# One-core attention and mixture-of-experts kernel: a token load, a late weight and leftover pair work change places at the start of the expert steps

## The reference

```python
q = relu(x @ Wq.T + bq); k = relu(x @ Wk.T + bk); v = x @ Wv.T + bv     # 16 heads of 16
q_ = concat([q * sin, q * cos]); k_ = concat([k * sin, k * cos])        # by position
kv = einsum('nld,nlm->ndm', k_, v)
z = 1.0 / maximum(einsum('nld,nd->nl', q_, k_.sum(axis=1)), 1e-4)
x = layernorm(x + (einsum('nld,ndm->nlm', q_, kv) * z) @ Wo.T + bo)
logits = x @ router_w.T; topv, topi = top_k(logits, 2); w = softmax(topv)
for e in range(8):
    out += gate[:, e:e+1] * (gelu(x @ w1[e].T) @ w2[e].T)               # 256 -> 512 -> 256
x = layernorm(x + out)
```

## Time and profile before

| what | value |
|---|---|
| median of 3 runs | 858.84 us (858.13 to 859.87) |
| the profiled execution | 858.07 us |
| its span, first to last instruction | 856.3 us |
| mean granted TensorE clock | 0.981 |
| PE busy | 800.6 us (93%) |
| DVE busy | 566.9 us (66%) |
| ACT busy | 460.2 us (54%) |
| POOL busy | 428.8 us (50%) |
| HBM traffic | 124 GB/s over the span |

### The profile page before, as it was taken

The page is one execution under the profiler, slowest core; times in us unless marked ns, Lnnn a source line. Parts: engine busy times, 40 slices in busy tenths (PEclk is TensorE's granted clock), DMA queues, the critical chain, the costliest instruction groups (busy, mean ns, idle before and its releaser), DMA issues.

```text
span 856.3 us, 22053 instructions
## 1 busy us (share of the span) xinstructions
PE 800.6 (93%) x6684; PEld 736.7 (86%) x6684; DVE 566.9 (66%) x1816; ACT 460.2 (54%) x1044; POOL 428.8 (50%) x545
## 2 busy tenths in 40 slices
PE   5999999999899869999999999999999999999990
PEld 4888999889899858999899999989999999999980
DVE  3336788878888766666766666664444477777773
ACT  3556676666766644445444544434444445566653
POOL 3886566666677663444445444553222234444442
PEclk9999999999999978999999999999999999999996
DMA  6444033333333242332333332232322355666644
GB/s 195 164 139 133 26 115 121 101 102 107 105 101 101 89 154 82 101 96 89 90 102 106 101 98 85 88 107 82 120 76 78 122 186 191 223 224 215 227 168 172
DMA packets 56469, 106.64 MB, mean 125 GB/s; under 512 B 9262, under 2 KB 37552, under 8 KB 54449
## 3 DMA queue, kind: packets, MB, share of 16 engines
q1 hardware_dynamic: 41296, 63.25, 25.0%
q0 software_dynamic: 12624, 33.84, 10.8%
q10 hardware_dynamic: 2448, 8.26, 2.6%
HBM read 61.91 MB, written 44.32 MB: 124 GB/s over the span
## 4 chain that ended last, share of the span: by engine, by line
PE 80%; DVE 6%; issue 5%; ACT 5%; DMA 3%; SPq 1%; POOL 1%; ACTq 0%; POOLq 0%; DVEq 0%
PE PS L736 23%; PE PS L724 22%; PE PS L540 10%; PE PS L754 7%; PE PS L577 4%; PE PS L713 4%; PE PS L613 4%; PE PS L629 3%; PE PS L600 1%; PE PS L560 1%; ACT vs L851 1%; DMA boc<-in_bo_columns 1%; ACT vs L850 1%; PE PS L547 1%; DVE o L1047 1%
## 5 line engine op out<-in xcount | busy, mean ns | idle before, releaser
L1670 POOL DMA_INDIRECT token_rows<-xg x135 | 134.8, 998 | 284.0 <-DVE xg L1403 261.6
L736 PEld LDWEIGHTS PS<-w,hT 128*128 128x128 f32 x1620 | 211.7, 189 | 13.5 <-issue 3.7
L724 PE MATMUL PS<-w,xgT 128*128 x810 | 222.9, 411 | 0.0
L736 PE MATMUL PS<-w,hT 128*128 x1620 | 218.3, 284 | 0.8 <-ACT hT L994 0.8
L724 PEld LDWEIGHTS PS<-w,xgT 128*128 128x128 f32 x810 | 143.8, 191 | 24.3
L1586 POOL DMA_INDIRECT expert_rows<-rows,idx x128 | 131.0, 1024 | 60.1 <-issue 35.4
L994 ACT ACTIVATE hT<-PS 128x512 fp32r<-128x512 f32 x135 | 80.7, 598 | 142.1 <-PE PS L754 138.4
L990 ACT ACTIVATE hg<-PS 128x512 f32<-128x512 f32 x135 | 80.5, 596 | 118.4 <-PE PS L724 106.4
L1468 DVE TENSOR_TENSOR hT<-PS,hT 128x512 fp32r<-128x512 f32 x135 | 93.4, 692 | 75.6 <-ACT hT L994 75.6
L1395 DVE TENSOR_TENSOR xgT<-PS,xgT 128x256 fp32r<-128x256 f32 x135 | 57.0, 422 | 75.6 <-ACT xgT L960 57.6
L754 PE MATMUL PS<-cst,hg 128*128 128x128 f32 x540 | 81.5, 273 | 0.7 <-ACT hg L990 0.7
(11 more groups left out here) (179 smaller groups left out, 1276.5 us busy)
## 6 DMA issues: line engine op xcount, KB each, us to landing
xg<-expert_rows SPq DMA_DIRECT2D x135, 130.0 KB
z<-token_rows SPq DMA_DIRECT2D x15, 1024.0 KB
xraw<-in_xT SPq DMA_DIRECT2D x32, 256.0 KB
xtok<-in_x SPq DMA_DIRECT2D x32, 256.0 KB
out_y<-z ACTq DMA_DIRECT2D x15, 512.0 KB, 3.2
wraw<-in_w1T SPq DMA_DIRECT2D x7, 512.0 KB, 3.8
wraw<-in_w2T SPq DMA_DIRECT2D x7, 512.0 KB, 3.6
token_rows<-xg POOLq DMA_INDIRECT x135
```

The costliest lines, as they stand in the source:

```text
L724: mm = nc.tensor.matmul(PS[:, gH, :], xgT[:, s % 2, a, k, :], w[:, bass.ds(e, 1), b, k * F:(k + 1) * F].rearrange("p o f -> p (o f)"), sta ...
L736: return nc.tensor.matmul(PS[:, gY, 0:D], hT[:, a, k, :], w[:, bass.ds(e, 1), b, HALF + k * D:HALF + (k + 1) * D] .rearrange("p o f -> p ( ...
L1670: nc.gpsimd.indirect_dma_start(yd, bass.IndirectOffsetOnAxis(ap=xg[:, XG_SLOTS[s % NXG], C_DST:C_GATE].bitcast(U32), axis=0), xg[:, XG_SLO ...
```

## The change

Nothing is added or left out of what is computed; only places in the engines' orders change.

- SP: `tokens(23)` moves from ahead of the late weight's first half to behind the eighth gather. In the steps, `tokens(j)` moves from hook place 0 to place 4.
- Last rep of the first phase: DVE does `positions(20)` and `attention_low(22)` at once, and `gates(20)`, `row_stats(21)`, `row_means(21)` and `logits(21)` move behind `rows_low(0)`. POOL does `late_weight` ahead of `half_deviation(21)`, and two of pair 20's four scatters move into steps 0 and 1.
- PE: `attend(23)`, second half, moves behind `hidden(0)`; `rank(21)`, `attention_transposed(23)`, `project_out(23)` and `rank(22)` each one step later.
- ACT: `normalise(21)` and the second cosine part move into step 0, `query_high(24)` into 1, `attention_high(23)` from 2 to 4, `normalise(22)` from 1 to 5, `normalise(23)` from 6 to 8.
- DVE: the blocks of pairs 21 to 23 that lay ahead of the steps and in steps 0 to 5 lie in steps 0 to 7; the `seg_start` part moves from step 5 to step 12.
- POOL: pair 21's scatters go from steps 1 to 4 to steps 3 to 6, the first two of pair 22 from 5 and 6 to 7 and 8, the deviations and gate powers one to three steps later.

```diff
@@ SP
-            tokens(GROUP_PAIRS - 1)
             sp.wait_ge(q_done, NPAIR)
             sp.dma_start(w_late_raw[:, 0, 1, 0:HALF], w_experts[0][EARLY]).then_inc(s_late[0], 16)
@@ SP, steps
             for s in range(FULL_STEPS):
-                if hook(s)[1] == 0 and s < LAST_GROUP:
+                if s == NXG:
+                    tokens(GROUP_PAIRS - 1)
+                if hook(s)[1] == 4 and hook(s)[0] is not None:
                     tokens(hook(s)[0])
@@ PE
             rows_transposed(0)
-            attend(A, G - 1, 1)
@@ PE, steps
                 hidden(s, now)
-                if s == 5:
+                if s == 0:
+                    attend(A, G - 1, 1)
+                if s == 6:
                     rank(A - 1, G - 1, A)
...
-                if s == 0:
+                if s == 1:
                     rank(A - 2, G - 2, A)
-                if s == 2:
+                if s == 3:
                     attention_transposed(A, G - 1)
-                if s == 4:
+                if s == 5:
                     project_out(A, G - 1)
@@ ACT
-            normalise(A - 2, (A - 2) // 2, True, 1)
-            nc.scalar.activation(gelu_first[:], half_neg[:, 0:2], ACT.Gelu, scale=2.0)
             act.wait_ge(s_late[0], 16)
             act.wait_ge(kv_done, 2 * NPAIR)
             nc.scalar.activation(w[:, EARLY, 0, 0:HALF], w_late_raw[:, 0, 1, 0:HALF], ACT.Copy).then_inc(late_high, 1)
             cos_part(A, G - 1, 0)
+            nc.scalar.activation(gelu_first[:], half_neg[:, 0:2], ACT.Gelu, scale=2.0)
...
             rows_high(0)
-            cos_part(A, G - 1, 1)
-            query_high(A + 1, A + 1 - GROUP_PAIRS, True)
@@ ACT, steps
+                if s == 0:
+                    cos_part(A, G - 1, 1)
+                    normalise(A - 2, (A - 2) // 2, True, 1)
                 if s == 1:
+                    query_high(A + 1, A + 1 - GROUP_PAIRS, True)
+                if s == 4:
+                    attention_high(A, G - 1)
+                if s == 5:
                     normalise(A - 1, (A - 1) // 2, True, 0)
-                if s == 2:
-                    attention_high(A, G - 1)
-                if s == 6:
+                if s == 8:
                     normalise(A, A // 2, True, 1)
@@ DVE, first phase
+                if rep == NPAIR - 1:
+                    dve.wait_ge(x1_ready, j - 1)
+                    positions(j - 2, slot)
+                    attention_low(j)
+                    return
@@ DVE
             state_out(B - 1, 2 * NPAIR)
-            choose(A - 2, G - 2, 1)
...
-            residual(A - 1, 0, (A - 1) // 2 * 16 + 16)
-            logits_sum(A - 1, 2 * ((A - 1) % LX))
             add_sin_part(A, G - 1, 0)
...
             rows_low(0)
-            row_stats(A - 1, 0)
-            row_means(A - 1, G - 2)
-            logits(A - 1)
-            add_sin_part(A, G - 1, 1)
-            gates(A - 2, G - 2, 1)
+            row_stats(A - 2, 1)
+            row_means(A - 2, G - 3)
+            logits(A - 2)
+            gates(A - 3, G - 3, 0)
@@ DVE, steps
                 if s == 0:
+                    choose(A - 2, G - 2, 1)
+                    add_sin_part(A, G - 1, 1)
+                if s == 1:
+                    state_split(B - 1)
+                if s == 2:
                     normalise_attention(A, G - 1)
-                    state_split(B - 1)
-                if s == 1:
+                    residual(A - 1, 0, (A - 1) // 2 * 16 + 16)
+                    logits_sum(A - 1, 2 * ((A - 1) % LX))
+                if s == 3:
+                    dve.wait_ge(x1_ready, A - 1)
+                    gates(A - 2, G - 2, 1)
                     positions(A - 2, 1)
-                if s == 2:
+                    row_stats(A - 1, 0)
+                if s == 4:
+                    row_means(A - 1, G - 2)
+                    logits(A - 1)
                     attention_low(A)
+                if s == 5:
+                    choose(A - 1, G - 1, 0)
                     query_low(A + 1, A + 1 - GROUP_PAIRS)
-                if s == 3:
-                    choose(A - 1, G - 1, 0)
-                    gates(A - 1, G - 1, 0)
-                if s == 4:
+                if s == 6:
                     residual(A, 1, A // 2 * 16 + 16)
                     logits_sum(A, 2 * (A % LX))
+                    dve.wait_ge(x1_ready, A)
+                    gates(A - 1, G - 1, 0)
+                    positions(A - 1, 0)
+                if s == 7:
                     row_stats(A, 1)
                     row_means(A, G - 1)
                     logits(A)
-                if s == 5:
-                    positions(A - 1, 0)
+                if s == FIRST_GROUP + GROUP - 1:
@@ POOL, first phase
+                if rep == NPAIR - 1:
+                    late_weight()
                 if onward:
                     half_deviation(j - 1)
...
                 if rep == NPAIR - 1:
-                    late_weight()
                     scattered(j - 2)
-                    for h in range(2):
-                        for k in range(TOPK):
-                            scatter(slot, h, k)
+                    scatter(slot, 0, 0)
+                    scatter(slot, 0, 1)
@@ POOL, steps
-            gate_power(A - 2)
-            half_deviation(A - 1)
...
-                if 1 <= s <= 4:
-                    if s == 1:
+                if s < 2:
+                    scatter(0, 1, s)
+                if s == 1:
+                    gate_power(A - 2)
+                if 3 <= s <= 6:
+                    if s == 3:
                         scattered(A - 2)
-                    scatter(1, (s - 1) // 2, (s - 1) % 2)
+                    scatter(1, (s - 3) // 2, (s - 3) % 2)
                 j, n = hook(s)
-                if s == 3:
+                if s == 4:
+                    half_deviation(A - 1)
+                if s == 5:
                     gate_power(A - 1)
...
+                if s == 7:
+                    half_deviation(A)
                 send(s)
-                if s == 4:
-                    half_deviation(A)
-                if 5 <= s <= 6:
-                    if s == 5:
+                if 7 <= s <= 8:
+                    if s == 7:
                         scattered(A - 1)
-                    scatter(0, 0, s - 5)
+                    scatter(0, 0, s - 7)
```

## The result

The changed kernel took **851.41 us** in the median of 9 runs, the kernel before 858.84: a ratio of 0.9926, with a 95% interval of 0.9908 to 0.9944. The profiled execution took 851.41 us, its span is 849.6 us at a mean granted clock of 0.984 (before: 858.07, 856.3, 0.981).

The account below looks back on a forecast made before the run. TensorE bounds the kernel, idle where attention ends and expert steps begin. 6.3 - 0.76 + 0.7 + 0.65 - 0.5 = 6.4 us off the median 858.84 gives 852.4 us; range 850.0 to 856.8.

Parts of the forecast that it names:

- The chain to the first expert product: Transition from attention to expert steps: earlier weight and gather bring the first expert product to 314.7 instead of 321.04.
- The scatter's completion: Pair 19's last scatter, which the first gather awaits: taken as complete at 309.5, bounds 309.0 and 311.7.
- the rival of the late confirmation: Scatter complete only at 311.7: transition slides 2.2 us, gain 4.2, 854.6 us; chance 22%.
- the estimate of 311.0: Scatter's completion with the skill's roughly 2 us, mostly write receipt, counted from data end; sum 1.5 us worse, 853.9 us.
- that term: Transition up to the first expert product, at 314.7 instead of 321.04: gain 6.3 us.
- Attention product: Pair 23's second half on TensorE moves behind the first expert product: 0.76 us given back.
- gelu gap: TensorE's 0.69 us wait for ScalarE's gelu, covered by the moved attention product: gain 0.7 us.
- clock: Half speed lasts 3.4 to 6.8 us behind the first expert product's start; middle cost 2.5: gain 0.65 us.
- stalls: Extra work spread over eight steps instead of six, TensorE gaps of at most 0.3 us: 0.5 us given back.
- The token load's place: Token loads at the fourth hook, not the zeroth: gathers no longer queue behind them; worth 0.
- my number for GpSimd's whole part of the weight: Late weight's second half on GpSimd: 3.9 us of its own after the last scatter, ending at 311.9.

Follow-up runs that it names:

- e6: Changed kernel without GpSimd's wait for the attention division ahead of pair 19's last two scatters, last rep only: 849.68 us, ratio 0.991.
- e2: Kernel before with only the late weight's first half loaded ahead of pair 23's token load: 854.41 us, ratio 0.9971.
- e3: Kernel before with late weight and gathers ahead of pair 23's token load, now behind seven gathers; other engines keep the old order: 855.84 us, ratio 0.9978.
- e4: Changed kernel with the late weight's first half loaded right behind the first gather: 857.9 us, ratio 1.0009.
- e8: Changed kernel with 32 small matmuls added on TensorE ahead of the first expert product, shifting its code: 852.8 us, ratio 0.9958.
- e10: Changed kernel with GpSimd's second scatter of pair 23's first half moved from step 8 to step 9: 846.66 us, ratio 0.9927.
- e5: Changed kernel with VectorE's state split moved back from step 1 to step 0: 854.39 us, ratio 0.9968.
- e9: Changed kernel with the steps' token load back at hook place 0 instead of 4: 854.86 us, ratio 1.002.
- e11: Changed kernel with pair 23's second-half attention product back ahead of the first expert product on TensorE: 846.1 us, ratio 0.9923.
- e7: e6 with ScalarE's gelu table loaded in the last rep and VectorE's sin part behind its first rows: 849.33 us, ratio 0.9914.
- e1: The changed kernel as it is, run and profiled again on another chip: 852.95 us, ratio 0.9945.
- e12: e7 with gather 0's transposes ahead of pair 22's output projection on TensorE: 851.02 us, ratio 0.9925.

## Why the prediction was right, and where it was not

**The chain to the first expert product** held link by link. Predicted and measured: weight issued 301.2 and 301.41; rounding 307.2 and 307.21; gather 310.6 and 310.66; transposes 312.7 and 312.84; product 314.7 and 314.84. The scatter's completion, which no row of before showed, is 309.6 where I took 309.5: SyncE's last wait ahead of the gathers, at the line of the earlier trace rows, now begins at 305.4 and lasts 4.23 us, and in e6, where the scatters go out earlier, 0.03 us:

```profile
L466 SPq EVENT_SEMAPHORE  x1: 4233/4233/4233, 305.4 to 305.4; - x1
```

That refutes the rival of the late confirmation and the estimate of 311.0 that I had drawn from the Trainium skill (DMA: Bandwidth & Descriptors, the anatomy of a GpSimd DMA); the receipt was in by 2.5 us after the scatter's issue at 307.12. e2, e3 and e4 show how the parts hang together. The early weight load is worth 2.9 us, the early gathers nothing on top of it, and the gathers with the other engines' new orders 3.1; with the weight late, all the rest is worth 1.7. What the old order leaves late once both loads are early is ScalarE's rounding of the weight as well as VectorE's extra blocks (e3).

**The size of that term**, 6.3, was 6.00. I had set 314.7 against 321.04, the product's place in the chain, where the timeline has the old product start at 320.69; two views of one instruction were mixed.

**Attention product, gelu gap, clock and stalls** were +0.09 us in my sum (0.76 back, 0.7 and 0.65 gained, 0.5 back). Steps 0 to 7 gained 1.27 - 0.19 = 1.08. I had half speed for a middle of 5 us behind the product's start, with 3.4 and 6.8 as its ends; the trace has 2.9, below the good end, and that is luck in part. In other traces with the gap for the gelu covered the clock rose 2.7 us (e8), 2.9 (e10), 4.2 (e5), 5.2 (e4) and 5.5 us (e9) behind the product, and with the gap open it rose after 7.4 (before) and 7.3 (e11), but also after 3.5 (e2) and 2.1 (e3). That the covered gap brings the rise forward is therefore not shown. Between e10 and e9, which have the same order there, steps 0 to 3 differ by 0.68 us. What I had booked as 0.76 back and 0.7 gained was worth 1.6 us together in e11 beside e10, the clock's share included. The stalls were as counted or less, none above 0.2 us in steps 0 to 8, and e5 shows what the alternative costs. The Trainium skill (TensorE: Matmul & The Clock Gate, HAM oscillation) warns of waits between groups of matmuls that bring half speed back. e5, with a wait of 1.82 us, and e9, with 5.52, agree; each fell once and did not oscillate.

**The token load's place** was 0 in my sum and is 0 against the kernel before. But my sentence did not say what it costs if left: the change moves pair 22's x1 from step 1 into step 5, and the load at the old place would have held gather 7 for it. That is 7.9 us (e9), more than the whole gain. The move of the load is what keeps this price away, and I had not written it down.

**The loss in steps 8 to 11**, 1.65 us, is the term that the prediction lacks. In sum the trace has 5.43 us up to step 12 where I had 6.4: 0.3 less up to the product, 1.0 more in steps 0 to 7, 1.65 less behind them. The trace and the forecast agree to 1.0 us in part because errors of opposite sign met, and the medians' gain, 7.4 us, lies on the other side of 6.4; that much agreement is luck. The loss has two parts. About 0.45 is a wait for VectorE's division in step 9, on all chips: e10 takes 4.35 us from step 9's product to step 10's, the kernel before 3.91. The other 1.2 us are in step 10. TensorE's row of four transposes ends at 360.07, but ScalarE starts on their result at 362.48, after a wait that the trace can put to no instruction ("remote"), and the next transposes but one wait for VectorE. Some 40 us later, at 404.3, ScalarE and VectorE both start late together, so it is not the queue of one of them. TensorE's timeline of the changed kernel, then ScalarE's and VectorE's:

```profile
355.89 0.66 PE L601 MATMUL PS<-cst,o 128*128 128x128 f32 x4 [0.19 <-DVE o L1062]
...
359.47 0.60 PE L755 MATMUL PS<-cst,hg 128*128 128x128 f32 x4
...
366.48 0.41 PE L714 MATMUL PS<-cst,xg 128*128 128x128 f32 x2 [0.94 <-DVE xgT L1401]
```
```profile
362.48 0.60 ACT L993 ACTIVATE hT<-PS 128x512 fp32r<-128x512 f32 x1 [3.37 <-remote]
...
404.31 0.60 ACT L993 ACTIVATE hT<-PS 128x512 fp32r<-128x512 f32 x1 [2.55 <-remote]
```
```profile
404.25 0.48 DVE L1409 SCALAR_TENSOR_TENSOR xg<-PS,xg 128x256 f32<-128x256 f32 x1 [2.04 <-remote]
```

What is ruled out: the position of TensorE's code (e7 and e8), VectorE's block of step 0 (e5), the hold (e6). What speaks for a cause, though no run tests it: in the traces of before, changed and e1 to e8, this late hand-over stands behind a pile of GpSimd's indirect transfers. In the changed kernel three in a row begin at 352.39 and three at 357.4; the old order has two in a row at most there, and no late hand-over. Some 40 us later every one of these traces, the old order too, has four in a row (403.69 before, 398.41 changed) and a hand-over 1.4 to 2.1 us late. e6, e7 and e12, whose GpSimd issues four in a row just ahead of the transition, have one of 2.0 us there (300.4 in e6), though TensorE's program is the same in e6 as in the changed kernel. On the chip of e9 to e11 no hand-over was late anywhere, with piles as large or larger, and the kernel before took 852.9 us there and 856.7 to 858.8 on the others. So the pile alone does not bring the delay about: the chip or its state has a part in it. Whether the pile is needed at all is not shown, since e10, which took it apart, ran on that chip. The cause stays open.

**The best version measured** is e6 or e7, ratios 0.991 and 0.9914; their intervals overlap with the changed kernel's. The traces have them 1.8 us ahead of it at step 12, and 1.2 to 1.3 ahead of e8, the changed order on their own chip. The late hand-over of 2.0 us ahead of the transition takes part of what they gain.

## What to carry to other kernels

When several engines meet at one product, cost each part of a change by what the others leave: here one load that stayed late took everything back (e4), and the early gathers alone gave nothing (e3). Where work moves to a later step, look through the queues for every load that waits for its result and for what is queued behind that load; that price (e9) can be larger than the gain. Compare traces by stretches between two events of one engine, not by the times of whole runs, which here spread by more than most of the effects, nor by times counted from the start of the span: e6's gather looks 3.7 us earlier so and is 1.95. And before a difference in the clock between two kernels is given a cause, look at how far it varies between traces of one order.

## What the runs showed of the hardware

- VectorE and GpSimd hold each other up on work with two inputs in SBUF. The subtraction of 128x1024 took 1.77 us in the changed kernel, where GpSimd's overlapped it, and 1.23 before and 1.22 in e6, where it did not; GpSimd's four took 3.63 us, and 3.67 in e6, where they overlapped other such work of VectorE's, beside 2.79 before. e4, the changed kernel with the subtraction late, is the control: 1.23 and 2.76. The Trainium skill (SBUF — State Buffer, Who interferes with whom) has the two engines lock a shared pair of ports; the direction agrees, but both sides grew, by 0.54 and 0.84 us. It cost nothing here: the gather landed at the time when GpSimd ended, 312.85. 3.9 us, my number for GpSimd's whole part of the weight, was 4.8.
- A wait of TensorE cost more than its length in the two runs where the clock fell with it: 1.82 us of waiting cost 3.55 (e5), 5.52 cost 7.9 (e9).
- The same order of work met the clock's rise 2.9 us (changed kernel, e10) and 5.5 us (e9) behind the first expert product's start.
- An engine can start on a result of TensorE up to 2.4 us (2.5 in e1) after the end that the profile gives its matmuls, with nothing in the rows to show why; three kernels of the new order on another chip (e9 to e11) did not have it.
